# Routed rows normalised on ScalarE instead of VectorE, with new instruction orders on four engines ahead of the experts

## The reference

```
h = patch_tokens(x)                 # 5 shifted copies, LayerNorm over 3840, projection to 192
h = concat([h, txt])
h = h + attn0(layernorm(h))         # 12 heads of 8, each of 4 segments of 24 tokens by itself
h = h + moe(layernorm(h))           # 8 experts, top 2, capacity 60 of 192 tokens, relu, 768 hidden
h = h + attn1(layernorm(h))         # linear attention, l1 norms
h = h + soft_moe(layernorm(h))      # 8 experts of 4 slots, gelu
```

## Time and profile before

| | |
|---|---|
| median of 3 runs | 353.85 us (352.6 to 359.36) |
| the profiled execution | 351.75 us, of which 349.9 us are the span of the trace |
| busy: TensorE, VectorE, ScalarE, GpSimd | 319.5, 193.6, 112.5, 52.4 us |
| granted TensorE clock, mean | 0.995 of full speed (2.4 GHz) |
| first expert matmul | 126.30 us |

### The profile page before, as it was taken

The page is one execution under the profiler, slowest core; times in us unless marked ns, Lnnn a source line. Parts: engine busy times, 40 slices in busy tenths (PEclk is TensorE's granted clock), DMA queues, the critical chain, the costliest instruction groups (busy, mean ns, idle before and its releaser), DMA issues.

```text
span 349.9 us, 9294 instructions
## 1 busy us (share of the span) xinstructions
PE 319.5 (91%) x3966; PEld 216.6 (62%) x3966; DVE 193.6 (55%) x636; ACT 112.5 (32%) x218; POOL 52.4 (15%) x100
## 2 busy tenths in 40 slices
PE   3999899887788889999999999999998999998595
PEld 3876468655665336574747484756676576777465
DVE  2817487999999992141431110202045887789864
ACT  1233635665741352222222213030202232333250
POOL 8403233100111000000020000000028811101100
PEclk9999999999999999999999999999999999999899
DMA  7985011333120000505050505000002200000005
GB/s 254 350 238 146 5 37 36 116 108 125 54 55 3 2 0 2 153 7 156 3 157 2 157 2 157 4 21 24 0 25 65 53 20 0 3 2 0 2 0 135
DMA packets 16485, 23.45 MB, mean 67 GB/s; under 512 B 3995, under 2 KB 12573, under 8 KB 16445
## 3 DMA queue, kind: packets, MB, share of 16 engines
q1 hardware_dynamic: 14972, 21.10, 20.1%
q0 software_dynamic: 576, 1.18, 1.3%
q10 hardware_dynamic: 896, 0.59, 0.7%
HBM read 20.11 MB, written 2.75 MB: 65 GB/s over the span
## 4 chain that ended last, share of the span: by engine, by line
PE 64%; DVE 16%; SPq 8%; issue 4%; DMA 3%; POOL 2%; ACT 2%; DVEq 0%; POOLq 0%
PE banks L755 18%; PE banks L770 18%; PE banks L810 3%; PE banks L264 3%; SPq L288 2%; PE banks L818 2%; SPq L340 2%; PE banks L654 2%; PE banks L857 2%; PE banks L847 2%; PE banks L522 2%; DVE sb_onehot_combT L1729 2%; DVE sb_stat L1551 2%; POOL sb_onehot_combT L478 2%; SPq L286 1%
## 5 line engine op out<-in xcount | busy, mean ns | idle before, releaser
L755 PE MATMUL banks<-sb_tok_xeT,sb_wi_sl 128*128 128x480 f32 (+1 forms) x192 | 64.9, 590 | 1.1 <-ACT sb_tok_xeT L1264 1.1
L770 PE MATMUL banks<-sb_wo_sl,sb_attn_hidT_attn 128*60 128x192 f32 x768 | 64.1, 327 | 0.0
L770 PEld LDWEIGHTS banks<-sb_wo_sl,sb_attn_hidT_attn 128*60 128x60 f32 x768 | 52.9, 133 | 12.5 <-issue 4.0
L1279 ACT ACTIVATE sb_attn_hidT_attn<-banks 128x480 f32<-128x480 f32 x48 | 25.6, 569 | 95.7 <-PE banks L755 95.7
L755 PEld LDWEIGHTS banks<-sb_tok_xeT,sb_wi_sl 128*128 128x128 f32 (+1 forms) x192 | 24.8, 187 | 37.7 <-issue 35.8
L1777 DVE COPY sb_w_tok_e_out<-banks 60x384 f32<-60x384 f32 x16 | 8.9, 555 | 61.9 <-PE banks L770 61.6
L522 PE MATMUL banks<-sb_tok_xeT 128*32 128x193 f32 (+1 forms) x512 | 23.4, 328 | 0.0
L1779 DVE COPY sb_onehot_combT<-banks 60x384 f32<-60x384 f32 x16 | 8.9, 555 | 22.1 <-PE banks L770 22.0
L522 PEld LDWEIGHTS banks<-sb_tok_xeT 128*32 128x32 f32 (+1 forms) x512 | 15.8, 109 | 5.9 <-issue 2.3
L810 PE MATMUL banks<-sb_w_kv,sb_xnT 96*128 96x384 f32 x48 | 17.6, 497 | 1.0 <-ACT sb_xnT L1290 1.0
L1183 ACT ACTIVATE sb_onehot_combT<-sb_tok_xeT 128x1024 f32<-128x1024 f32 x8 | 8.5, 1059 | 21.7 <-DMA sb_tok_xeT<-in_xhalo 21.7
(11 more groups left out here) (262 smaller groups left out, 516.9 us busy)
## 6 DMA issues: line engine op xcount, KB each, us to landing
sb_wo_sl<-in_wo SPq DMA_DIRECT2D x8, 576.0 KB, 4.7
sb_tok_xeT<-in_xin SPq DMA_DIRECT2D x8, 448.0 KB, 5.4
sb_wi_sl<-in_wi SPq DMA_DIRECT2D x8, 288.0 KB, 3.1
sb_wi_sl<-in_wi SPq DMA_DIRECT2D x24, 96.0 KB, 3.1
sb_w_tok_e_out<-in_wtok SPq DMA_DIRECT2D x2, 960.0 KB, 7.2
expert_rows<-sb_onehot_combT SPq DMA_DIRECT2D x8, 192.0 KB, 4.4
sb_w_tok_e_out<-in_wtok SPq DMA_DIRECT2D x1, 576.0 KB, 8.4
out<-sb_h SPq DMA_DIRECT2D x8, 72.0 KB, 2.0
```

The costliest lines, as they stand in the source:

```text
L755: mm = nc.tensor.matmul(PS[:, banks[z], 0:SLOTS], lhs, rhs.rearrange("k g c -> k (g c)"), start=first, stop=not first)
L770: mm = nc.tensor.matmul(PS[64 * z:64 * z + CAP, 4 + hf, pr * D:(pr + 1) * D], hidT[:, e % 2, f, g * CAP:(g + 1) * CAP], wo_sl[:, q, f], st ...
L1279: nc.scalar.activation(hidT[:, e % 2, f], PS[:, HID_BANKS[(e * (FT // 2) + f // 2) % 2][f % 2], 0:SLOTS], ACT.Relu).then_inc(sem("hidT"), 1)
```

## The change

`route_norm(j)` moves from VectorE to ScalarE. It becomes an Identity activation per block with a scale and a bias per row: `h * rs_r + shift_r`. The shift, minus the mean times the scale, is new work for GpSimd, two operations of 128x3 per group (`route_scale`), and ScalarE waits for it (`r_shift_of`). `scale_routes` on VectorE still waits for `rs_r` alone.

At the same time the lists of calls of TensorE, ScalarE, VectorE and GpSimd up to the experts are laid anew. No call is added or dropped but those of `route_norm`. After the experts' start the lists are the same as before. The core of the diff:

```diff
@@ build @@
         rs_r = sb("rs_r", [128, J, NB])
+        shift_r = sb("shift_r", [128, J, NB])
@@ GpSimd @@
+            def route_scale(j):
+
+                norm_scale("r", j, rs_r[:, j], mv_r[:, j])
+                then(gp.tensor_scalar(shift_r[:, j], mv_r[:, j, :, 0], -1.0, None, ALU.mult))
+                gp.wait_ge(sem("r_rs"), j + 1)
+                gp.tensor_tensor(shift_r[:, j], shift_r[:, j], rs_r[:, j], ALU.mult).then_inc(sem("r_shift_of"), 1)
+
             token_scale(0)
             token_scale(1)
+            token_scale(2)
             norm_scale("a", 0, rs_a[:, 0], mv_a[:, 0])
-            token_scale(2)
...
-            norm_scale("r", 0, rs_r[:, 0], mv_r[:, 0])
...
+            route_scale(0)
...
@@ TensorE @@
             weight_sums()
             patches(1, 0)
             free(sums=1)
+            spread_sums()
             square_rows(0)
-            spread_sums()
+            patches(1, 1)
+            free(x_ss=1)
+            square_rows(1)
             square_sums(0)
-            square_rows(1)
-            patches(1, 1)
+            free(x_ss=2)
+            square_rows(2)
+            square_sums(1)
             free(tok_mid=2, tok_var=2)
             patches(2, 0)
-            square_sums(1)
+            patches(2, 1)
+            free(x_ss=3)
+            square_rows(3)
...
@@ ScalarE @@
+            def route_norm(j):
+                act.wait_ge(sem("r_shift_of"), j + 1)
+                for blk in range(NB):
+                    nc.scalar.activation(xn2[:, j, blk], h[:, j, blk], ACT.Identity, bias=shift_r[:, j, blk:blk + 1],
+                                         scale=rs_r[:, j, blk:blk + 1]).then_inc(sem("r_xn"), 1)
+
...
             keep_queries(2)
             keep_keys(2)
+            route_norm(0)
             keep_weights(1, 0)
-            keep_weights(1, 1)
             keep_values(2, 0)
             keep_values(2, 1)
+            keep_weights(1, 1)
...
@@ VectorE @@
-            def route_norm(j):
-                ve.wait_ge(sem("r_rs"), j + 1)
-                normalize("r_xn", j, xn2[:, j], mv_r[:, j], rs_r[:, j])
-
...
-            add_attention(0)
-            route_moments(0)
-            route_logits(0)
-            choose_first(0)
-            choose(0)
-            scale_routes(0)
             score_max(1, 0)
             score_max(1, 1)
-            first_norm(3)
             score_norm(1, 0)
             score_max(1, 2)
             score_norm(1, 1)
             score_norm(1, 2)
+            add_attention(0)
+            route_moments(0)
+            route_logits(0)
+            choose_first(0)
+            choose(0)
+            scale_routes(0)
+            first_norm(3)
...
             place(0)
             mark_slots(0)
-            route_norm(0)
...
```

More of the change, by code:

```diff
@@ L928, in _ @@
             turn_inputs(0)
-            patches(2, 1)
+            square_sums(2)
+            free(tok_mid=4, tok_var=4)
+            turn_projection()
             free(a_xnT=1)
             reduce_inputs(0)
-            square_rows(2)
+            free(tok_mid=6, tok_var=6)
+            patches(3, 0)
+            free(a_xl=1, a_xrT=1)
+            keys(0)
+            patches(3, 1)
+            route_projection()
             queries(0)
-            free(a_xl=1)
-            keys(0)
-            free(a_qT=1)
+            square_sums(3)
+            free(w_px=2)
+            scores(0)
             values(0, 0)
-            square_sums(2)
-            square_rows(3)
-            free(tok_mid=6, tok_var=6)
-            scores(0)
+            free(tok_mid=8, tok_var=8)
             values(0, 1)
@@ L945, in _ @@
             free(a_vexp=2)
-            patches(3, 0)
-            patches(3, 1)
-            free(x_ss=4)
-            turn_weights(0, 0)
-            turn_weights(0, 1)
-            square_sums(3)
-            free(a_sub=3)
-            turn_projection()
-            free(a_probT=1)
-            turn_weights(0, 2)
-            route_projection()
-            free(tok_mid=8, tok_var=8)
             values(0, 3)
@@ L960, in _ @@
             turn_inputs(1)
-            free(a_probT=2)
-            weigh_values(0)
+            turn_weights(0, 0)
             free(a_xnT=2)
             reduce_inputs(1)
-            free(a_oT=1)
-            project(0)
+            turn_weights(0, 1)
             queries(1)
@@ L971, in _ @@
             values(1, 0)
+            free(a_probT=1)
+            turn_weights(0, 2)
+            free(a_vexp=4)
             values(1, 1)
+            free(a_sub=3)
             scores(1)
@@ L975, in _ @@
             values(1, 2)
+            free(a_probT=2)
+            weigh_values(0)
             free(a_vexp=6)
@@ L979, in _ @@
             turn_inputs(2)
-            free(a_vexp=8)
-            count_choices(0)
+            free(a_oT=1)
+            project(0)
             free(a_xnT=3)
             reduce_inputs(2)
-            free(a_h=1)
-            turn_weights(1, 0)
             queries(2)
@@ L1005, in _ @@
             turn_inputs(3)
+            free(a_vexp=12)
+            count_choices(0)
+            free(a_xnT=4)
+            reduce_inputs(3)
             free(a_oT=2)
             project(1)
-            free(a_xnT=4)
-            reduce_inputs(3)
             queries(3)
@@ L1012, in _ @@
             keys(3)
+            free(a_qT=4)
+            values(3, 0)
             free(a_h=2)
@@ L1024, in _ @@
             free(a_vexp=13)
-            values(3, 2)
+            dispatch(0)
             free(a_probT=8)
             weigh_values(2)
+            free(r_counted=1)
+            values(3, 1)
+            free(a_oT=3)
+            project(2)
+            free(xeT=2)
+            values(3, 2)
             free(a_vexp=14)
             values(3, 3)
-            free(a_oT=3)
-            project(2)
-            free(a_vexp=15)
-            dispatch(0)
             free(a_h=3)
@@ L1410, in _ @@
             exp_scores(3, 1)
-            keep_values(3, 2)
+            keep_dispatched(0)
             keep_outputs(2)
             exp_scores(3, 2)
+            keep_values(3, 1)
+            keep_values(3, 2)
             keep_values(3, 3)
-            keep_dispatched(0)
             keep_weights(3, 0)
             keep_weights(3, 1)
+            exp_routes(1)
             keep_weights(3, 2)
+            route_norm(2)
+            keep_outputs(3)
             exp_routes(2)
-            keep_outputs(3)
             keep_dispatched(1)
+            route_norm(3)
             keep_tails(0)
@@ L1940, in _ @@
             token_write(0)
+            token_rows(2)
             token_write(1)
@@ L1943, in _ @@
             head_values()
+            token_write(2)
+            token_rows(3)
             first_norm(0)
[L1945 to L1947 removed]
             token_write(3)
             first_moments(1)
[L1950 removed]
             token_rows(4)
             token_rows(5)
+            first_norm(1)
             token_write(4)
+            token_write(5)
+            first_moments(2)
+            keep_projection()
+            token_rows(6)
+            token_rows(7)
             score_max(0, 0)
             score_max(0, 1)
+            score_norm(0, 0)
             score_max(0, 2)
[L1957 to L1959 removed]
             score_norm(0, 1)
             score_norm(0, 2)
[L1962 to L1963 removed]
+            first_norm(2)
             token_write(6)
[L1965 removed]
             token_write(7)
[L1967 removed]
             first_moments(3)
+            score_max(1, 0)
+            score_max(1, 1)
+            score_norm(1, 0)
+            score_max(1, 2)
+            score_norm(1, 1)
+            score_norm(1, 2)
             add_attention(0)
```

103 lines of the change are left out of this document (40 added, 63 removed).

## The result

The changed kernel takes 356.32 us (median of 13 runs, 354.5 to 359.67), the kernel before 353.93 us (13 runs). The ratio is 1.008, with a 95% interval of 1.005 to 1.011: slower by 0.8%, where I had forecast no change. The profiled execution took 355.48 us, with a span of 353.7; that of before had 351.75 and 349.9. Of the 3.8 us between the spans, 3.90 lie ahead of the first expert matmul (130.20 against 126.30).

A forecast was written before the change was run, and what follows sets the result against it. VectorE's unbroken 58.38 us stretch was taken to set the experts' start. Removing 3.5 us and starting 3.45 us later gave 64.75 + 54.9 = 119.65 against 119.69: no change, 353.8 us, eight-in-ten range 350 to 357.5.

The forecast's parts named there:

- part 1: VectorE's stretch before the experts: four route_norm calls, 3.5 us, leave it; its work falls from 58.38 to 54.9 us.
- the tail: From keep_tails(0) to the first expert matmul: 6.6 us in both kernels.
- (a): Early TensorE: square_sums(0) starts at 30.2, not 26.31; image 6 is issued 1.5 us later, near 30.4.
- (c): Group 3's patches now precede scores(0): score_max(0, 0) at 52.8, 7.0 us later; VectorE stands about 5 us at keep_projection.
- (d): From score_max(0, 0) at 52.8 to score_max(1, 0) at 64.75: VectorE waits 1.7 us, its stretch starts 3.45 us later.
- (b): TensorE after group 2's patches: waits 1.6 us for squares of images 6 and 7; reduce_inputs(0) at 41.3, before 37.85.
- Covers in the full stretch: VectorE's stretch before the experts: TensorE stays ahead by 0.3 to 2.4 us at each handover, so VectorE never waits.
- A: Rival: early part shorter than walked, VectorE's stretch starts at 61.4, removal counts in full: 350.5 us; chance 0.30.
- B: Rival: ScalarE's queue stands at route_norm, delaying project(2) and project(3): +3, 356.8 us; chance 0.15.
- C: Rival: GpSimd's eight new operations of 0.24 us hold VectorE up in its stretch: +1.9, 355.7 us; chance 0.05.
- D: Rival: VectorE is not what ends last once it has less work, so the gain is smaller; no chance of its own.
- ScalarE's price: Twelve 128x192 activations of 0.32 us, about 1 us per route_norm, some 4 in all, taken from 27 us idle.

The follow-up runs named there:

- the kernel after again: The changed kernel measured once more, unaltered: 356.98 us (4 runs, too few for an interval).
- the run with the orders alone: Changed kernel with the normalisation back on VectorE and GpSimd's shift dropped, new orders of all engines kept: 362.95 us, ratio 1.022 to the kernel before.
- the run with doubled work: Changed kernel with every activation of route_norm made twice on ScalarE: 357.13 us, ratio 1.007 to the kernel before.
- my own first placing: Kernel before with only the normalisation moved, old orders, route_norm(0) between exp_scores(1, 2) and keep_queries(2): 353.24 us, ratio 0.996.
- placed: Normalisation alone moved, old orders, route_norm(0) ahead of keep_reduced(2), route_norm(1) one call earlier: 351.84 us, ratio 0.988; again 351.09 us, 0.994.
- the kernel before again: The kernel before measured once more, unaltered: 354.2 us.
- the run with (a) undone: Changed kernel with square_sums(0) again ahead of patches(1, 1), and keep_squares(0) ahead of squares(4): 355.34 us, ratio 1.002 to the kernel before.

## Why the prediction was wrong

**What bounds the kernel, part 1 and the tail held.** VectorE's stretch sets the start of the experts: the tail behind it was 6.60 or 6.61 us in both kernels and in every variant up to the experts' start. The stretch without the removed work was 55.1 us at its cleanest (66.39 to 121.47, the kernel after again), against 54.9 forecast and 58.38 before, so 3.3 of the 3.5 us came.

**Parts (a), (c) and (d) held in their mechanisms.** `square_sums(0)` came at 29.87 for 30.2, image 6 was issued at 30.28 for 30.4, VectorE stood 5.51 us for about 5 at `keep_projection`, and from `score_max(0, 0)` to `score_max(1, 0)` there were 12.04 us for 11.95.

**The first step that failed is the start of the stretch, mis-sized above all in (b): 3.45 us forecast, 4.47 in the profile.** Image 7 came 0.4 us later than my 1.5 allowed, `reduce_inputs(0)` 0.73, and `scores(0)` 0.94 with a pause of 0.38 for which I had no row. So 0.73 us of the miss arose in (b), 0.21 in (c) and 0.09 in (d). The start was 65.78 for 64.75, 4.47 us later than before and not 3.45. In four executions with these orders it was 64.26, 65.28, 65.78 and 66.39, with image 7's square between 36.41 and 37.91; in five with the old ones it was 61.3 to 62.0, and in one 62.96 (the run with the orders alone is left out, its clock was low all through). The middle of each is 65.5 and 61.7, so the start costs 3.8 against 3.3 gained.

**The second step that failed is "Covers in the full stretch": that VectorE waits for nobody there, where the profile has waits of 2.60 us.** My covers of 0.3 to 2.4 us were worked out from one execution in which TensorE's pauses were hidden and its clock never fell. In the new order the pause of `weigh_values(0)` lies in front of an exponential with no cover (1.55 us in the profile, 0.96 in the run with doubled work, none in four others), and in group 3's routing `mark_slots(2)` waits for `dispatch_tails(0)` when the clock has fallen (1.05, 1.11 and 0.19 us in three of six executions). Such waits hit the old orders as well (0.30 to 1.71 us): summed over the stretch, and without those that the place of `route_norm(0)` made, they are 0 to 2.6 us in six executions of the new orders and 0 to 2.4 in six of the old, about 1 us on average in both. They explain the distance between the two profiles, but not that between the medians. None of my rivals was about them.

**The rivals.** A did not come: the start is nowhere near 61.4, though most of TensorE's wait of 1.08 to 1.95 us for image 7 goes when (a) is undone, near the 1.6 that I had put on that one DMA. B did not come in the kernel after: with twice the work on ScalarE `add_attention(2)` and `(3)` still had no wait. It did come in my own first placing, in another spot (in front of `keep_queries(2)`). C did not show: VectorE's small operations take about 183 ns with the eight new ones of GpSimd as before, and those took 0.25 and 0.19 us, the product a little below what I took. By the rule of the Trainium skill (SBUF — State Buffer, "Who interferes with whom"), under which the one that comes second is blocked, either engine could have paid. The trace shows no such price on VectorE. On GpSimd's side it has a case that fits, ahead of the full stretch: the operation at 34.74 took 0.78 us in place of 0.23, while VectorE worked on two SBUF inputs at 34.56 (0.53 us) and 35.01 (0.41 us). D is out: the move gains by itself.

**ScalarE's price** was too low, and hidden. A `route_norm` takes 1.42 us, not 1.0; the shift was there 4.1 us after the start of `add_attention` in all four groups, as forecast.

Most of the loss stays open. The later start less the work removed makes 0.5 us, and the waits add nothing on average, while the medians differ by 2.4. At equal mean clock (below) the kernel after is 0.5 to 3.1 us slower than the one before. That the new orders lose is shown by undoing them; how the loss splits is not. Whether the new orders bring more falls of the clock, or the rest is chance, these runs don't tell.

## What to carry to other kernels

A gain on the engine that bounds a stretch is lost if the same edit lets that stretch begin later: put both ends of the stretch into the sum, and undo the two halves of such a change one by one. An operation moved to an engine with much idle time costs what stands behind it in that engine's queue, so put it in front of the instruction before which that engine was idle: here three calls earlier in the queue took a wait of 1.07 us down to 0.17 in all three executions. A profile with no wait in a stretch is one execution; before slacks of a microsecond are relied on, see whether the clock or the pauses of another execution eat them.

## What the runs showed of the hardware

**The time follows TensorE's granted clock from run to run.** Median times of the runs that count in the ratios, by the mean granted clock of the run (to 0.001; in brackets how many; the kernel before has two more, at 0.971, and its runs come from three rounds, those of the kernel after mostly from another):

| mean clock | before | after | placed |
|---|---|---|---|
| 0.976 | 355.00 (5) | 358.10 (5) | none |
| 0.981 | 354.70 (22) | 356.50 (3) | 353.12 (1) |
| 0.985 | 354.35 (15) | 354.86 (6) | 352.25 (9) |
| 0.990 | 352.34 (11) | none | 349.31 (3) |
| 0.995 | 351.54 (5) | 353.29 (1) | 350.53 (4) |

The profile that I forecast from was of the last row. Falls came both behind a wait of TensorE (0.96 us ending at 110.12 in the kernel after, 1.59 at 107.26 in the kernel before again) and without one: in both looks at the run with (a) undone the clock fell between 50 and 52 us, behind 10 us in which TensorE had no wait but the 0.38 before `scores(0)`.

**An activation with a scale and a shift per row costs more than its width.** 192 columns from SBUF to SBUF take 534 ns (median in the kernel after), 0.44 us from start to start, while an exponential of 384 columns takes 523 and one of 24 columns 226. A table of the Trainium skill (VectorE: DVE Perf Modes, "The TRN2 errata — SBUF-src ops pay a fixed extra latency per instruction") gives 224 cycles and one per column at 1.2 GHz, 347 ns for 192 columns; the two exponentials come within 20 ns of it (507 and 207), this activation is 187 ns above it. Whether the scale, the shift or the form of the function makes the difference was not measured.

**TensorE's pauses stand at fixed instructions, and end 1 to 1.7 us after an instruction transfer.** In `weigh_values(0)` of the new orders they stand after 40 of 96 matmuls, in `weigh_values(1)` of the old after 26; their length goes from 0.3 to 2.8 us. The page of the kernel after has a DMA queue of the kind "instruction", and one of its transfers lies in the window 67.4 to 68.5 us, inside the pause of 66.96 to 69.73:

```profile
q8 instruction: 31, 0.51, 0.6%
...
q8 instruction: 1, 0.02, 5.8%
```

Every execution has 31 transfers of 16 KB on it. Between 60 and 126 us the 14 traces hold 24 pauses of 0.28 us or more that end with "issue", and in each of them TensorE goes on 0.98 to 1.67 us after the end of the queue's last transfer, though the transfers lie 3 to 20 us apart (in the kernel after 67.44 to 68.46, then TensorE at 69.73; in the kernel before 78.89 to 80.09, then 81.43). Most transfers have no pause behind them. So the pauses go with the fetch of instructions; that the transfer brings the very instruction at which TensorE stands is an inference. The Trainium skill (Runtime: NRT & Kernel Launch, "Instruction fetch mechanics") describes such a fetch by blocks and says that it is hidden; in these 24 places the trace differs. Why a transfer starts as late as it does was not looked into.
